# First norm of a frame normalised on ScalarE as one multiply-add a tile, its bias made by GpSimd

## The chip, the cores and the metric

The kernel runs on one core of one Trainium2 chip. The metric is the device time of one execution in microseconds (us); lower is better. Beside the plain runs there is one profiled execution, from which all rows below are taken. Engines are written as the profile writes them: PE is TensorE's matmul side and PEld its weight loads, DVE is VectorE, ACT is ScalarE, POOL is GpSimd, SP is SyncE; "PEq", "ACTq", "SPq" are the sequencers of these engines, which issue DMAs.

## What is computed

A gated cross-attention block with a mixture of experts behind it, on 2 x 1024 tokens of width 256 (2048 rows), against 154 context rows for each batch, 16 heads of 16 columns, 8 experts of which each token takes 2. Cut to what matters here:

```python
def _layernorm(x, eps=1e-05):
    m = jnp.mean(x, axis=-1, keepdims=True); v = jnp.var(x, axis=-1, keepdims=True)
    return (x - m) / jnp.sqrt(v + eps)

# first half: the norm whose normalising step is changed is the inner one here
x = x + jnp.tanh(g_xattn[0]) * attention(_layernorm(x), ctx, ctx, mask, Wq, bq, Wk, bk, Wv, bv, Wo, bo)
# second half: sigmoid router, top 2 of 8 experts, GELU layers 256 -> 1024 -> 256, weighted sum
x = x + jnp.tanh(g_ffn[0]) * experts(_layernorm(x), Wg, W1, b1, W2, b2)
```

## The kernel before

The 2048 rows are 16 tiles of 128 rows; two tiles make a **unit**, so there are U = 8 units, numbered 0 to 7. The program has three stages: a setup (weights turned, keys and values made, first units begun), ten **frames** of attention, and the expert stage, which takes 39 groups of 128 gathered tokens.

Every engine has its own instruction stream, written by hand; semaphores tie them. Nothing is reordered by a compiler, so what stands behind a waiting instruction on its engine waits with it. The loop is `for u in FRAMES: for i in range(ITEMS)` on each engine, with ITEMS = 10 items a frame. Frame u does the softmax of unit u (item i: one pair of heads), the maxima of unit u+1, the output projection and second norm of unit u-1, the router logits of unit u-2, and the first norm and query of unit u+3. The work of several units is so laid side by side in one frame.

The first norm of a unit has three parts. VectorE makes mean and variance (`first_moments`, lines 679 and 682). GpSimd makes 1/sqrt(var + eps) from them by an add and a power (`first_rstd`, lines 379 and 381). VectorE then subtracts the mean and multiplies (`layernorm1`, line 688, two instructions of 128 x 256 a unit), which gives `xn`. TensorE turns `xn` (`turn_x`, line 1088), ScalarE copies the turned tile out (`evacuate_x`, line 508), and TensorE multiplies by the query weights (`query`, line 1096). ScalarE and VectorE write the query's high and low halves (lines 515 and 715), and DMAs stack them for the score matmuls.

Moments and 1/sqrt are made in groups: `FIRST_NORMS = [(0,), (1, 2, 3)] + [(u,) for u in range(4, U)]`. Unit 0 and units 1 to 3 come in the setup; unit u+4 has its 1/sqrt made in frame u, one frame before its norm. `layernorm1` is called in the setup for units 0, 1, 2 and, in frames 0 to 4, at item 4 for units 3 to 7.

GpSimd's stream in the setup, around `first_rstd(1)`, stacks the keys for the scores, eight small DMAs for the high halves and eight for the low ones:

```python
stack_keys(pool, 1, kh, range(8), kst_pool_landed)
first_rstd(1)
pool.wait_ge(kv_made, 2 * KC)
stack_keys(pool, 2, kl, range(8), kst_pool_landed)
load(1)
```

The first score matmul (`max_scores(0, 0)`, line 1075) waits for these (`kst_pool_landed`) and for the query's DMAs (`qst_landed`), which ScalarE issues in the setup behind `evacuate_x(1)` (line 280).

In the frames ScalarE does, item by item, the exponential of the scores (line 583), and between them the copies out of PSUM and the high halves of the expert weights (`weights_high`, line 493); VectorE makes the low halves (`weights_low`, line 788), row maxima (line 722), their negative (`negate_maxima`, line 730), the division by the softmax sums (`weigh_values`, lines 699 and 700), and the residual update (line 878) behind the output projection (line 1246). GpSimd issues the loads of the expert weights (`load`, line 390) and adds the output bias to x (line 420).

Of the kernel before, what the change touches and what calls it, by code (L numbers as in the profile page):

```python
# [12 lines left out]
P = 128  # L13
F32, F16, I32, U8 = mybir.dt.float32, mybir.dt.float16, mybir.dt.int32, mybir.dt.uint8
ALU = mybir.AluOpType
# [11 lines left out]
def build(nc, x, ctx, mask, g_xattn, g_ffn, wq, bq, wk, bk, wv, bv, wo, bo, wg, w1, b1, w2, b2, out):  # L27
# [40 lines left out]
    with es:  # L68
# [46 lines left out]
        with ExitStack() as es_tail:  # L115
            outer, es = es, es_tail
            WT_qo = sb("WT_qo", [P, 2, KC, D])
            outT = sb("outT", [P, 2, 2 * UT])
            attn, attnT = sb("attn", [P, 2, D]), sb("attnT", [P, 2, KC, P])
            xn2 = attn  # L120
            xn2T = attnT
            stats, mv = sb("stats", [P, 2, 6]), sb("mv", [P, 2, 2])
            var, rstd = sb("var", [P, 2]), sb("rstd", [P, 2])
            recip = sb("recip", [P, 2, N_HEADS])


            with ExitStack() as es_attn:
                es = es_attn
                qst_spare = sb("qst2", [P, NPAIR, UT], F16)
                qh, ql = sb("qh", [P, KC, UT], F16), sb("ql", [P, KC, UT], F16)  # L130
                xn = sb("xn", [P, 2, D])
                xnT = xn
                kst = sb("kst", [P, B, NPAIR, 2, SP], F16)
                kst_late.append(sb("kst_late1", [P, NPAIR, 2 * (SP - P)], F16))
                v_a.append(sb("v_a1", [P, N_HEADS, VC]))
                v_b.append(sb("v_b1", [P, 4, 4, VC]))
                qst = [sb(f"qst{i}", [P, NPAIR, UT], F16) for i in range(2)] + [qst_spare]
                mv1, rstd1 = sb("mv1", [P, T, 2]), sb("rstd1", [P, T])
                rowmax, negmax = sb("rowmax", [P, 2 * N_HEADS]), sb("negmax", [P, 2 * N_HEADS])
                negmaxT = sb("negmaxT", [2 * N_HEADS, P], F16)  # L140
                probs = sb("probs", [P, 3, 2, UT])


            with ExitStack() as es_route:
                es = es_route
                ahead = sb("ahead", [P, T, E, E], F16)
                sig, gate_rows, rank = sb("sig", [P, T, E]), sb("gate_rows", [P, T, E]), sb("rank", [P, T, E])
                chosen16, chosen = sb("chosen16", [P, T * E], F16), sb("chosen", [P, TOP_K, T, E])
                sb("first_ranks_end", [P, 8192 - 2048 - 3 * 512 - 256 - 1024], U8)
                at_place, tab_rhs = sb("at_place", [P, TOP_K * T, P], F16), sb("tab_rhs", [P, TOP_K * T, TAB], F16)  # L150
                before, ones = sb("before", [P, P], F16), sb("ones", [P, P], F16)
                iota_slot, iota_tile = sb("iota_slot", [P, P], F16), sb("iota_tile", [P, TAB], F16)
                token_no, spare_row = sb("token_no", [P, TOP_K * T]), sb("spare_row", [P, 1])
                picked = sb("picked", [P, TOP_K, T, E])
                n_int, n_tiles, tile_end, tile_base, no_add = (sb("n_int", [P, E], I32), sb("n_tiles", [P, E]), sb("tile_end", [P, E]),
                                                                sb("tile_base", [P, E]), sb("no_add", [P, E]))
                pos_f, local_f, place_f, base_f, tile_f, place_neg = (sb(n, [P, TOP_K, T]) for n in (
                    "pos_f", "local_f", "place_f", "base_f", "tile_f", "place_neg"))
                token_neg = sb("token_neg", [P, TOP_K * T])
                pos_i, local_i, place_i = (sb(n, [P, TOP_K, T], I32) for n in ("pos_i", "local_i", "place_i"))  # L160
                empty, token_m1 = sb("empty", [P, TAB]), sb("token_m1", [P, TAB])
                past, begun = sb("past", [P, TAB, E], F16), sb("begun", [P, TAB, E], F16)
                expert_f = sb("expert_f", [1, TAB])
                b2_rows = sb("b2_rows", [P, E, D])
            es = outer
# [23 lines left out]
        bo_gated = sem("bo_gated")  # L189
        dve_step = sem("dve_step")  # L190
        ln1_done, x_biased = sem("ln1_done"), sem("x_biased")
        moments1_made, var1_made, rstd1_made = sem("moments1_made"), sem("var1_made"), sem("rstd1_made")
        neg_half_made, v_zeroed = sem("neg_half_made"), sem("v_zeroed")
        moments_made, var_made, rstd_made = sem("moments_made"), sem("var_made"), sem("rstd_made")
# [154 lines left out]
        def _(pool):  # L349
# [25 lines left out]
            def first_rstd(n):  # L375
                units = FIRST_NORMS[n]
                tiles = slice(2 * units[0], 2 * units[-1] + 2)
                pool.wait_ge(moments1_made, n + 1)
                nc.gpsimd.tensor_scalar(var1[:, tiles], mv1[:, tiles, 1], EPS, None, ALU.add).then_inc(var1_made, 1)
                pool.wait_ge(var1_made, n + 1)  # L380
                nc.gpsimd.tensor_tensor(rstd1[:, tiles], var1[:, tiles], neg_half[:, 0:2 * len(units)], ALU.pow).then_inc(rstd1_made, 1)

            pool.wait_ge(neg_half_made, 1)
            first_rstd(0)
# [24 lines left out]
            for n, (_, high, low) in enumerate(chunks):  # L409
# [6 lines left out]
                if n in bias_at:  # L416
                    u = bias_at[n]
                    pool.wait_ge(bo_gated, 1)
                    pool.wait_ge(ln1_done, u + 1)
                    nc.gpsimd.tensor_tensor(x_unit(u), x_unit(u),  # L420
                                            bias_o[:, :].unsqueeze(1).broadcast_to([P, 2, D]), ALU.add).then_inc(x_biased, 1)
                if n < SETUP_CHUNKS:
# [56 lines left out]
        def _(act):  # L479
# [7 lines left out]
            def weights_high(n):  # L487

                if n == E * KC:
                    act.wait_ge(x2_stored, 16 * 3)  # L490
                    pass
                act.wait_ge(w_staged[n % 2], 16 * (n // 2 + 1))
                ins = nc.scalar.activation(chunks[n][1], W_stage[n % 2][:, :], ACT.Copy, scale=W_SCALE)  # L493
                if n < SETUP_CHUNKS:
                    ins = nc.scalar.activation(W_stage[n % 2][:, :], W_stage[n % 2][:, :], ACT.Copy, scale=W_SCALE)
                ins.then_inc(w_high, 1)

            def evacuate_values(v, n):
                act.wait_ge(pv_done, ITEMS * v + 5 * (n + 1))
# [76 lines left out]
            for u in FRAMES:  # L576
                for i in range(ITEMS):
# [16 lines left out]
                    if i == 1 and live(u - 2):  # L594
                        v = u - 2
                        act.wait_ge(q_filled, q_nth["logits", v])
                        nc.scalar.activation(Z[:, 2 * v:2 * v + 2, :].rearrange("p j e -> p (j e)"), Q_BANK[:, 0:2 * E],
                                             ACT.Exp, scale=-1.0).then_inc(q_free, 1)
                    if i == 4 and live(u - 1):
                        v = u - 1  # L600
                        act.wait_ge(a_filled, a_nth["attnT", v])
# [60 lines left out]
        def _(dve):  # L662
# [187 lines left out]
            for u in FRAMES:  # L850
                for i in range(ITEMS):
# [7 lines left out]
                    if i == 3 and live(u - 1):  # L859
# [8 lines left out]
                        for j in range(2 if v == U - 1 else 0):  # L868
                            dve.wait_ge(last_turned, j + 1)
                            weigh_values(j, LAST_TURN[j], xn).then_inc(last_weighed, 1)  # L870
                    if i == 4 and live(u + 3):
                        layernorm1(u + 3)
                    if i == 5 and live(u - 1):
                        v = u - 1
                        dve.wait_ge(q_filled, q_nth["wo", v])
# [127 lines left out]
        def _(pe):  # L1003
# [78 lines left out]

            def turn_x(v):
                a_use("xT", v)
                pe.wait_ge(ln1_done, v + 1)
                for c in range(KC):
                    for j in range(2):
                        ins = nc.tensor.transpose(A_BANK[:, c * UT + j * P:c * UT + (j + 1) * P], xn[:, j, c * P:(c + 1) * P], ident[:, :])
# [300 lines left out]
```

## Time and profile before

| | |
|---|---|
| median of 3 runs | 473.85 us (471.4 to 474.21) |
| the profiled execution | 474.62 us |
| its span, first to last instruction | 472.5 us |
| mean granted TensorE clock | 0.931 |
| busy: PE, DVE, ACT, POOL | 402.3, 313.5, 226.3, 174.6 us |

The setup ends at about 48 us of the span, the frames run from there to about 215 us, routing to 237 us, and the expert stage fills the rest. A row of the timeline gives start, length, engine, line, operation, `out<-in`, how many instructions were merged, and in brackets how long the engine sat idle before it and what released it. The chain is the sequence of work that ended last, traced back from the end.

### The profile page before, as it was taken

Reading aid. Unit: us, or ns where it says so; the run is one execution under the profiler, and the core shown is the slowest. Engines: PE = TensorE matmul, PEld = TensorE weight load, DVE = VectorE, ACT = ScalarE, POOL = GpSimd, SP = SyncE. Lnnn points to the kernel's source line nnn. Section 1 sums busy time; section 2 is a strip of 40 time slices with the busy share of each in tenths; the row PEclk is TensorE's granted clock in tenths of the full one; section 3 lists DMA queues with packets and bytes.
Section 4 is the critical chain, followed back from the end, with each engine's and each line's share of the span. In section 5 each row is a group of like instructions: output and inputs, shape, how many; then the busy total and the mean of one; then the engine's idle time right before and its main releaser. Section 6 shows DMA issues by size and latency. Waiting matters only on the chain.

```text
span 472.5 us, 11085 instructions
## 1 busy us (share of the span) xinstructions
PE 402.3 (85%) x4018; PEld 319.1 (68%) x4018; DVE 313.5 (66%) x833; ACT 226.3 (48%) x576; POOL 174.6 (37%) x193
## 2 busy tenths in 40 slices
PE   5848988988989888975259999999999999999980
PEld 3623445554555544544259999999999999999970
DVE  4666776968777586688826667666666666665650
ACT  2244664656555465646235544544454454443530
POOL 8624642223222131210043444454544445444331
PEclk9985898999999899987559999999999999999996
DMA  7463353525353433442011332322333222233311
GB/s 217 101 184 113 124 155 112 175 100 168 100 163 107 153 108 130 135 141 84 4 52 23 56 57 49 46 47 49 49 54 58 46 51 46 47 49 46 46 24 22
DMA packets 35300, 41.27 MB, mean 87 GB/s; under 512 B 10461, under 2 KB 29777, under 8 KB 35121
## 3 DMA queue, kind: packets, MB, share of 16 engines
q0 software_dynamic: 12608, 27.48, 25.0%
q1 hardware_dynamic: 20113, 12.22, 8.9%
q10 hardware_dynamic: 2528, 0.87, 0.8%
q8 instruction: 33, 0.54, 0.5%
q14 instruction: 18, 0.15, 0.1%
HBM read 26.90 MB, written 9.50 MB: 77 GB/s over the span
## 4 chain that ended last, share of the span: by engine, by line
PE 69%; DVE 15%; DMA 5%; ACT 5%; issue 3%; POOLq 0%; ACTq 0%; SPq 0%; POOL 0%; DVEq 0%
PE bank L1309 7%; PE bank L1310 7%; PE bank L1311 7%; PE bank L1323 7%; PE bank L1324 7%; PE bank L1325 7%; PE bank L1058 6%; PE bank L1075 4%; DVE rowmax L722 3%; PE bank L1246 3%; PE bank L1096 3%; DMA out_rows<-y_sb,scatter_tab 2%; PE bank L1278 2%; DVE W L788 2%; PE bank L1214 2%
## 5 line engine op out<-in xcount | busy, mean ns | idle before, releaser
L1309 PE MATMUL bank<-xh,W 128*128 128x128 f16 x624 | 121.8, 221 | 0.9 <-DVE xl L953 0.9
L1310 PE MATMUL bank<-xl,W 128*128 128x128 f16 x624 | 121.7, 221 | 0.0
L1311 PE MATMUL bank<-xh,W 128*128 128x128 f16 x624 | 121.7, 221 | 0.0
L647 ACT ACTIVATE h<-bank,b1T 128x128 f32<-128x128 f32 x312 | 88.9, 368 | 58.7 <-PE bank L1311 56.1
L459 POOL DMA_INDIRECT out_rows<-y_sb,scatter_tab x39 | 62.2, 1594 | 108.6 <-DVE y_sb L982 99.4
L1323 PE MATMUL bank<-W,hh 128*128 x312 | 85.1, 273 | 1.1 <-DVE hl L964 1.1
L1324 PE MATMUL bank<-W,hh 128*128 x312 | 85.0, 273 | 0.0
L1325 PE MATMUL bank<-W,hl 128*128 x312 | 85.0, 273 | 0.0
L722 DVE TENSOR_REDUCE rowmax<-bank 128x2 f32<-128x308 f32 x128 | 57.1, 472 | 25.7 <-PE bank L1075 24.8
L962 DVE CAST hh<-h 128x512 f16<-128x512 f32 x78 | 33.5, 430 | 47.5 <-ACT h L647 46.7
L1309 PEld LDWEIGHTS bank<-xh,W 128*128 x624 | 61.7, 99 | 4.3 <-DVE xl L953 1.3
L1310 PEld LDWEIGHTS bank<-xl,W 128*128 x624 | 61.7, 99 | 3.4
L583 ACT ACTIVATE probs<-bank 128x512 f32<-128x512 f32 x80 | 47.3, 596 | 32.7 <-PE bank L1180 21.1
L1311 PEld LDWEIGHTS bank<-xh,W 128*128 x624 | 61.7, 99 | 0.0
L964 DVE TENSOR_TENSOR hl<-h,hh 128x512 f16<-128x512 f32 x78 | 54.0, 692 | 2.7
L390 POOL DMA_DIRECT2D W_stage<-in_L_ffn_W x32 | 21.7, 679 | 83.4 <-DVE W L788 82.2
L451 POOL DMA_INDIRECT xg<-xn_scratch,gather_tab x39 | 39.2, 1004 | 35.5 <-DVE gather_tab L940 17.0
L1075 PE MATMUL bank<-kst,qst 97*128 97x308 f16 x128 | 39.9, 329 | 10.1 <-DVE rowmax L722 6.7
L629 ACT ACTIVATE xh<-bank 128x256 f16<-128x256 f32 x39 | 14.9, 383 | 67.4 <-PE bank L1278 67.3
L1058 PE MATMUL bank<-probs,v_a 128*32 128x256 f32 x256 | 40.7, 398 | 4.5 <-ACT probs L583 4.2
L1075 PEld LDWEIGHTS bank<-kst,qst 97*128 97x128 f16 x128 | 12.3, 100 | 35.3 <-DVE rowmax L722 21.8
L788 DVE SCALAR_TENSOR_TENSOR W<-W_stage,W 128x1024 f16<-128x1024 f32 x28 | 34.0, 1218 | 2.9 <-ACT W L493 2.9
(178 smaller groups left out, 655.4 us busy)
## 6 DMA issues: line engine op xcount, KB each, us to landing
W_stage<-in_L_ffn_W POOLq DMA_DIRECT2D x32, 512.0 KB, 4.0
xn_scratch<-attn SPq DMA_DIRECT2D x8, 256.0 KB, 2.2
qst<-qh SPq DMA_DIRECT2D x60, 32.0 KB, 2.4
X_late<-in_x SPq DMA_DIRECT2D x6, 256.0 KB, 6.7
out_rows<-X_late SPq DMA_DIRECT2D x6, 256.0 KB, 2.5
b_rows<-in_L_ffn_b SPq DMA_DIRECT2D x1, 1024.0 KB, 4.8
qst<-ql SPq DMA_DIRECT2D x28, 32.0 KB, 3.1
xg<-xn_scratch,gather_tab POOLq DMA_INDIRECT x39, 2.9
```

What stands on the lines that cost most here:

```text
L459: nc.gpsimd.indirect_dma_start(out=out, out_offset=bass.IndirectOffsetOnAxis(ap=scatter_tab[:, t:t + 1], axis=0), in_=y_sb[t % 3][:, :], i ...
L647: ins = nc.scalar.activation(h32[s % 4][:, m * P:(m + 1) * P], H_BANKS[s % 4][:, m * P:(m + 1) * P], ACT.Gelu_apprx_tanh, scale=1.0 / W_SC ...
L722: nc.vector.reduce_max(rowmax[:, 2 * n:2 * n + 2], S1_BANKS[g % 2][:, 0:2 * S].rearrange("p (a s) -> p a s", a=2), AX_X).then_inc(rowmax_d ...
L964: nc.vector.tensor_tensor(hl[s % 4][:, :], h32[s % 4][:, :], hh[s % 4][:, :], ALU.subtract).then_inc(hl_made, 1)
L1058: ins = nc.tensor.matmul(dst, lhs, rhs, start=(i % 5 == 0 and a == 0), stop=(i % 5 == 4), skip_group_check=True)
L1075: nc.tensor.matmul(S1_BANKS[g % 2][:, 0:2 * S].rearrange("p (a s) -> p a s", a=2), qst[v % 3][0:ROW_MAX, p, j * P:(j + 1) * P], kst[0:ROW_ ...
L1309: nc.tensor.matmul(dst, wh, xh[t % 3][:, cut], start=(c == 0), stop=False)
L1310: nc.tensor.matmul(dst, wh, xl[t % 3][:, cut], start=False, stop=False)
L1311: ins = nc.tensor.matmul(dst, wl, xh[t % 3][:, cut], start=False, stop=(c == KC - 1))
L1323: nc.tensor.matmul(y, hh[s % 4][:, cut], both[0], start=(m == 0), stop=False)
L1324: nc.tensor.matmul(y, hh[s % 4][:, cut], both[1], start=False, stop=False)
L1325: ins = nc.tensor.matmul(y, hl[s % 4][:, cut], both[0], start=False, stop=(m == FC - 1))
```

## The change

For units 3 to 7, the units that are normalised in the frames, the normalising step leaves VectorE (item 4) and becomes two ScalarE activations a unit behind the exponential of item 2: Identity(rstd * x + shift), with shift = -mean * rstd, one multiply-add a tile of 128 x 256. GpSimd makes shift: in each of the five `first_rstd` calls that hold such a unit it gets two operations more, a negation of the means and a product with rstd. Units 0 to 2 are normalised by VectorE as before. The waits for the finished norm follow the new semaphore.

```diff
+                mean_neg, shift1 = sb("mean_neg", [P, T]), sb("shift1", [P, T])
...
@@ -377,8 +379,14 @@
                 tiles = slice(2 * units[0], 2 * units[-1] + 2)
                 pool.wait_ge(moments1_made, n + 1)
                 nc.gpsimd.tensor_scalar(var1[:, tiles], mv1[:, tiles, 1], EPS, None, ALU.add).then_inc(var1_made, 1)
+                if units[-1] >= 3:
+                    nc.gpsimd.tensor_scalar(mean_neg[:, tiles], mv1[:, tiles, 0], -1.0, None, ALU.mult).then_inc(mean_negated, 1)
                 pool.wait_ge(var1_made, n + 1)
                 nc.gpsimd.tensor_tensor(rstd1[:, tiles], var1[:, tiles], neg_half[:, 0:2 * len(units)], ALU.pow).then_inc(rstd1_made, 1)
+                if units[-1] >= 3:
+                    pool.wait_ge(rstd1_made, n + 1)
+                    pool.wait_ge(mean_negated, sum(m[-1] >= 3 for m in FIRST_NORMS[:n + 1]))
+                    nc.gpsimd.tensor_tensor(shift1[:, tiles], mean_neg[:, tiles], rstd1[:, tiles], ALU.mult).then_inc(shift1_made, 1)
 
             pool.wait_ge(neg_half_made, 1)
             first_rstd(0)
@@ -416,7 +424,10 @@
                 if n in bias_at:
                     u = bias_at[n]
                     pool.wait_ge(bo_gated, 1)
-                    pool.wait_ge(ln1_done, u + 1)
+                    if u < 3:
+                        pool.wait_ge(ln1_done, u + 1)
+                    else:
+                        pool.wait_ge(ln1_late_done, u - 2)
                     nc.gpsimd.tensor_tensor(x_unit(u), x_unit(u),
                                             bias_o[:, :].unsqueeze(1).broadcast_to([P, 2, D]), ALU.add).then_inc(x_biased, 1)
                 if n < SETUP_CHUNKS:
@@ -494,6 +505,14 @@
                 if n < SETUP_CHUNKS:
                     ins = nc.scalar.activation(W_stage[n % 2][:, :], W_stage[n % 2][:, :], ACT.Copy, scale=W_SCALE)
                 ins.then_inc(w_high, 1)
+
+            def first_norm(v):
+                act.wait_ge(q_filled, q_nth["q", v - 1])
+                act.wait_ge(shift1_made, sum(m[-1] >= 3 for m in FIRST_NORMS[:first_norm_of[v]]))
+                for j in range(2):
+                    t = 2 * v + j
+                    ins = nc.scalar.activation(xn[:, j, :], x_unit(v)[:, j, :], ACT.Identity, scale=rstd1[:, t:t + 1], bias=shift1[:, t:t + 1])
+                ins.then_inc(ln1_late_done, 1)
 
             def evacuate_values(v, n):
                 act.wait_ge(pv_done, ITEMS * v + 5 * (n + 1))
@@ -596,6 +615,8 @@
                         act.wait_ge(q_filled, q_nth["logits", v])
                         nc.scalar.activation(Z[:, 2 * v:2 * v + 2, :].rearrange("p j e -> p (j e)"), Q_BANK[:, 0:2 * E],
                                              ACT.Exp, scale=-1.0).then_inc(q_free, 1)
+                    if i == 2 and live(u + 3):
+                        first_norm(u + 3)
                     if i == 4 and live(u - 1):
                         v = u - 1
                         act.wait_ge(a_filled, a_nth["attnT", v])
@@ -868,8 +889,6 @@
                         for j in range(2 if v == U - 1 else 0):
                             dve.wait_ge(last_turned, j + 1)
                             weigh_values(j, LAST_TURN[j], xn).then_inc(last_weighed, 1)
-                    if i == 4 and live(u + 3):
-                        layernorm1(u + 3)
                     if i == 5 and live(u - 1):
                         v = u - 1
                         dve.wait_ge(q_filled, q_nth["wo", v])
@@ -1082,7 +1101,10 @@
 
             def turn_x(v):
                 a_use("xT", v)
-                pe.wait_ge(ln1_done, v + 1)
+                if v < 3:
+                    pe.wait_ge(ln1_done, v + 1)
+                else:
+                    pe.wait_ge(ln1_late_done, v - 2)
                 for c in range(KC):
                     for j in range(2):
                         ins = nc.tensor.transpose(A_BANK[:, c * UT + j * P:c * UT + (j + 1) * P], xn[:, j, c * P:(c + 1) * P], ident[:, :])
```

Three places show what stands in each stream; names before `<-` are tiles written, behind it those read.

GpSimd in the setup, from the stacking of the high key halves (`kst<-kh`) to the next weight load, first before, then changed:

```order
L269 DMA kst<-kh 16x4x154 x8
L379 TENSOR_SCALAR var<-mv 128x6
L381 TENSOR_TENSOR rstd<-var,neg_half 128x6
L269 DMA kst<-kl 16x4x154 x8
L390 DMA W_stage<-in_L_ffn_W 128x1024
```

```order
L271 DMA kst<-kh 16x4x154 x8
L381 TENSOR_SCALAR var<-mv 128x6
L383 TENSOR_SCALAR mean_neg<-mv 128x6
L385 TENSOR_TENSOR rstd<-var,neg_half 128x6
L389 TENSOR_TENSOR shift<-mean_neg,rstd 128x6
L271 DMA kst<-kl 16x4x154 x8
L398 DMA W_stage<-in_L_ffn_W 128x1024
```

One operation now stands ahead of the power and one between it and the eight DMAs of the low key halves.

ScalarE in frame 2, from the weight piece of item 0 to the exponential of item 4 (`probs<-bank` is an exponential, `Z<-bank` the router's), first before, then changed:

```order
L493 ACTIVATE W<-W_stage 128x1024
L583 ACTIVATE probs<-bank 128x512
L597 ACTIVATE Z<-bank 128x16
L583 ACTIVATE probs<-bank 128x512 x2
L493 ACTIVATE W<-W_stage 128x1024
L583 ACTIVATE probs<-bank 128x512
```

```order
L504 ACTIVATE W<-W_stage 128x1024
L602 ACTIVATE probs<-bank 128x512
L616 ACTIVATE Z<-bank 128x16
L602 ACTIVATE probs<-bank 128x512
L514 ACTIVATE xn<-X_late,shift,rstd 128x256 x2
L602 ACTIVATE probs<-bank 128x512
L504 ACTIVATE W<-W_stage 128x1024
L602 ACTIVATE probs<-bank 128x512
```

The pair of the norm stands between the exponentials of items 2 and 3, which were neighbours.

VectorE in frame 2, items 3 to 5, first before, then changed:

```order
L730 TENSOR_SCALAR negmax<-rowmax 128x32
L699 RECIPROCAL recip<-bank 128x16
L700 TENSOR_TENSOR attn<-bank,recip 128x256
L699 RECIPROCAL recip<-bank 128x16
L700 TENSOR_TENSOR attn<-bank,recip 128x256
L688 TENSOR_SCALAR xn<-X_late,mv,rstd 128x256 x2
L788 SCALAR_TENSOR_TENSOR W<-W_stage,W 128x1024
L878 SCALAR_TENSOR_TENSOR X_early<-bank,tanh_g,X_early 128x512
```

```order
L751 TENSOR_SCALAR negmax<-rowmax 128x32
L720 RECIPROCAL recip<-bank 128x16
L721 TENSOR_TENSOR attn<-bank,recip 128x256
L720 RECIPROCAL recip<-bank 128x16
L721 TENSOR_TENSOR attn<-bank,recip 128x256
L809 SCALAR_TENSOR_TENSOR W<-W_stage,W 128x1024
L897 SCALAR_TENSOR_TENSOR X_early<-bank,tanh_g,X_early 128x512
```

The weight piece follows the division directly; nothing ahead of it has moved.

## Rows read from the trace of the kernel before

**Rows 1.** Stretches of two frames: busy us (instructions), granted clock, DMA share, GB/s

```profile
68.00:89.00 21.00, 18.36 (x109) 10.70 (x109) 16.17 (x39) 11.35 (x20) 5.10 (x9) 0.92 0.46 139
89.00:110.00 21.00, 18.56 (x127) 11.57 (x125) 16.43 (x40) 12.78 (x24) 4.98 (x9) 1.00 0.42 135
```

**Rows 2.** The chain that ended last in frame 3: start, length, what

```profile
118.05 0.43 DVE attn L700
...
120.14 1.94 PE bank L1246 x8
```

**Rows 3.** Timeline of VectorE in frames 0, 1 and 3

```profile
63.34 0.48 DVE L722 TENSOR_REDUCE rowmax<-bank 128x2 f32<-128x308 f32 x1 [1.93 <-PE bank L1075]
...
79.97 0.75 DVE L878 SCALAR_TENSOR_TENSOR X_early<-bank,tanh_g,X_early 128x512 f32<-128x512 f32 x1 [3.50 <-PE bank L1246]
...
118.39 0.72 DVE L688 TENSOR_SCALAR xn<-X_late,mv,rstd 128x256 f32<-128x256 f32 x2
...
122.10 0.75 DVE L878 SCALAR_TENSOR_TENSOR X_late<-bank,tanh_g,X_late 128x512 f32<-128x512 f32 x1 [1.85 <-PE bank L1246]
```

**Rows 4.** Timeline of ScalarE: exponential of item 3 in frames 0, 1, 4

```profile
53.57 0.60 ACT L583 ACTIVATE probs<-bank 128x512 f32<-128x512 f32 x1 [0.55 <-PE bank L1180]
...
71.59 0.60 ACT L583 ACTIVATE probs<-bank 128x512 f32<-128x512 f32 x1 [1.56 <-PE bank L1180]
...
136.44 0.60 ACT L583 ACTIVATE probs<-bank 128x512 f32<-128x512 f32 x1 [1.42 <-PE bank L1180]
```

**Rows 5.** ScalarE's groups by line and shape: busy us, mean ns

```profile
L515 ACT ACTIVATE qh<-bank,bias_q 128x256 f16<-128x256 f32 x16 | 6.7, 471 | 10.3 <-DMA qst<-ql 8.1 <-PE bank L1096 2.2
...
L528 ACT ACTIVATE at_place<-at_place,token_no,token_neg 128x128 f16<-128x128 f16 x12 | 4.8, 482 | 0.0
...
L608 ACT ACTIVATE at_place<-iota_slot,place_neg 128x128 f16<-128x128 f16 x12 | 3.6, 388 | 3.0 <-DVE local_f L765 3.0
```

**Rows 6.** Timeline of ScalarE: the query's high halves in frame 3

```profile
127.92 0.83 ACT L515 ACTIVATE qh<-bank,bias_q 128x256 f16<-128x256 f32 x2
```

**Rows 7.** Timeline of PE in frame 0, at the turn of the maxima

```profile
57.00 0.27 PE L1107 MATMUL bank<-ident,negmax 128*32 128x128 f32 x1 [0.72 <-DVE negmax L730]
```

**Rows 8.** Timeline of GpSimd in the setup

```profile
20.45 0.27 POOL L379 TENSOR_SCALAR var<-mv 128x6 f32<-128x6 f32 x1
20.80 1.36 POOL L381 TENSOR_TENSOR rstd<-var,neg_half 128x6 f32<-128x6 f32 x1
22.13 4.28 POOL L269 DMA_DIRECT2D kst<-kl  x8
```

**Rows 9.** Timeline of VectorE in the setup: the norm of unit 1

```profile
22.27 0.73 DVE L688 TENSOR_SCALAR xn<-X_early,mv,rstd 128x256 f32<-128x256 f32 x2 [2.43 <-POOL rstd L381]
```

**Rows 10.** The chain from unit 1's norm to the first score matmul

```profile
21.30 1.73 PE bank L1144 x8
...
23.15 0.64 PE bank L1088 x4
...
26.03 3.85 DMA qst<-ql
...
29.93 0.32 PE bank L1075
```

**Rows 11.** Tile kst, the last key DMA (`kst<-kl`) alone: time to landing

```profile
DMA to landing us min/median/max: 3.8/3.8/3.8
```

**Rows 12.** Tile negmax (ns min/median/max), then timelines of VectorE and GpSimd

```profile
L730 DVE TENSOR_SCALAR negmax<-rowmax x8: 180/181/1302, 43.8 to 181.2; 128x32 f32<-128x32 f32 x8
...
55.55 1.30 DVE L730 TENSOR_SCALAR negmax<-rowmax 128x32 f32<-128x32 f32 x1
...
55.53 1.27 POOL L420 TENSOR_TENSOR X_early<-X_early,bias_o 128x512 f32<-128x512 f32 x1
...
116.33 0.72 POOL L381 TENSOR_TENSOR rstd<-var,neg_half 128x2 f32<-128x2 f32 x1
```

**Rows 13.** The chain in frame 1: the output projection

```profile
76.73 3.22 PE bank L1246 x8
```

More of the change, by code:

```diff
@@ L191, in build @@
         ln1_done, x_biased = sem("ln1_done"), sem("x_biased")
+        mean_negated, shift1_made, ln1_late_done = sem("mean_negated"), sem("shift1_made"), sem("ln1_late_done")
         moments1_made, var1_made, rstd1_made = sem("moments1_made"), sem("var1_made"), sem("rstd1_made")
```

## The prediction

> **What bounds the kernel now.** I read the chain of work that ended last first, to see which engine's work sets the end of a frame; then the timelines of VectorE and ScalarE at the two places that the change touches, to see what each waits for there; then GpSimd's timeline in the setup, since two of the new operations stand ahead of DMAs. The ten frames run at about 21 us each [rows 1]. In frame 3 the chain goes over VectorE's division, PE's output projection and back to VectorE's residual update [rows 2]. PE is busy 18.4 to 18.6 of 21 us in these stretches, VectorE 16.2 to 16.4 and ScalarE 11.4 to 12.8 [rows 1], and no engine is full: what counts is each hand-over. Everything up to the expert stage is one chain, so a delay that lies on it moves the end by its own length, and one that lies beside it by nothing. The reader is to see in the rows that both the place that loses the norm and the place that gains it are places where the engine waits for PE.
>
> **VectorE loses ten instructions.** Five pairs, 0.72 us a pair as it stands in the timeline [rows 3], the one at 118.39: 5 x 0.72 = 3.6 us less of VectorE's work. In frame 3 only the weight piece and the residual update come behind it, and the update finds VectorE idle for 1.85 us until PE's output projection ends; in frame 1 it is 3.50 us [rows 3]. The projection hangs on the division, which ends at 118.48 [rows 2] and stands ahead of the norm. So the idle time grows from 1.85 to about 2.6 us and nothing else starts earlier but the weight piece and the weight load behind it. Frame 0 has no division; there the next wait for PE behind the norm is 1.93 us [rows 3]. Gain: 0, in all five frames. What would be late next if the norm did count is the same projection, so nothing is hidden behind it.
>
> **ScalarE gains ten instructions.** No row shows this form (two operands by partition, 128 x 256). The nearest one with two such operands is 128 wide and takes 482 ns; with one operand it is 388 ns at 128 wide and 471 ns at 256 [rows 5], so 128 columns more cost 83 ns. One instruction: 482 + 83 = 565 ns. Two in a row overlap: 2 x 471 = 942 ns are 0.83 us in the timeline [rows 6], 0.11 us less. The pair: 2 x 565 - 110 = 1020 ns, and the next instruction waits some 0.11 us less than that, so ScalarE is held for 0.9 to 1.0 us. The bounds are 0.83 us (the query's pair, one operand fewer) and 1.2 us (565 ns each with no overlap, rounded up). It stands where ScalarE waits for PE: before the exponential of item 3 ScalarE is idle for 1.56 us in frame 1 and 1.42 us in frame 4 [rows 4], frames 2 and 3 lying between. In these four frames 1.42 - 1.2 leaves at least 0.2 us even at the upper bound: cost 0. In frame 0 the idle time is 0.55 us [rows 4], so that exponential comes 0.3 to 0.65 us late, 0.4 taken. What waits for it is PE's value matmul of item 4 and then the turn of the maxima, before which PE is idle for 0.72 us, waiting for VectorE's negation [rows 7]. Cost in frame 0: 0, up to 0.1 if the end of the range and all hand-overs add up. None of the waits that the new pair adds is late: its shift was made one frame earlier (unit 3's in the setup), and the query before it ended in the frame before.
>
> **GpSimd gains ten instructions.** In the frames GpSimd's own next step is a weight load that waits for VectorE's low half, so its two small operations (0.27 us is the one at 128 x 6 [rows 8]) cost nothing there. In the setup they stand in the way twice.
>
> First, the negation comes between the add and the power. The add starts at 20.45 and the power at 20.80, with 0.35 us between them for a 0.27 us operation and its semaphore [rows 8]. The negation fills part of that gap: two operations at some 0.21 us each reach to 20.87, with the semaphore at most to 21.07. The power and all behind it come 0.07 to 0.27 us later, 0.13 taken. VectorE's norm of unit 1 waits for the power (2.43 us [rows 9]) and ends at 23.00; PE's turn starts at 23.15, 0.15 us behind, and its previous matmul ended at 23.03 [rows 10]. So PE's turn was tied to both, and now follows the norm: the chain is 0.13 us later at ScalarE's four DMAs of the query's low half, the last of which lands at 26.03 + 3.85 = 29.88, and PE's first score matmul starts at 29.93 [rows 10].
>
> Second, the product stands ahead of the eight DMAs of the low key halves. It takes between 0.27 us (the add at the same shape) and 1.36 us (the power at the same shape) [rows 8]; a product is nearer to the add, and with its semaphore I take 0.4. These DMAs come 0.13 + 0.4 = 0.5 us later, 0.3 to 1.7 at the bounds. The eight were issued from 22.13 on in 4.28 us [rows 8], the last of them at 22.13 + 7/8 x 4.28 = 25.9; it landed 3.8 us later [rows 11], at 29.7, 0.2 us before the query's. Now it lands at 30.2, where the query's lands at 30.0. PE's first score matmul goes from 29.93 to about 30.25: cost 0.3 us. Bounds: 0.1 (the queues are full at that time and the 512 KB weight load behind comes later too, which may give it back) and 1.5 (1.7 - 0.2).
>
> **The sum.** 0 on VectorE, 0 on ScalarE, +0.3 in the setup: 474.62 + 0.3 = 474.9 us against the profiled execution. That execution lies 0.8 us above the median of the runs, 473.85, so the forecast for a median is 473.85 + 0.3 = 474.15, rounded to **474.2 us**. A measurement of this kernel can hardly tell less than 1% (4.7 us) from no change, since its three runs lie 2.8 us apart.
>
> **The rivals.**
>
> *Slower: the key DMAs set the start of the scores.* It is the second step of the setup at its upper end. If the product on GpSimd costs what the power does, 1.36 us, the DMAs come about 1.65 us later and land 1.45 us behind the query's. Every tenth from the point where the delay passes 0.2 us is a tenth on the end: 474.2 - 0.3 + 1.5 = 475.4. For it: the slack is only 0.2 us [rows 10, 11]. Against: a power is a long operation by itself. Chance 0.1.
>
> *Slower: GpSimd in VectorE's way.* In the one place where VectorE's negation (0.18 us in the median of its eight) was to start beside GpSimd's bias operation, at 55.55, it took 1.30 us and ended with that operation [rows 12]. In frames 1 to 3 the power now ends about when the negation starts: in frame 3 at 117.05 [rows 12], ahead of the division at 117.43 to 118.48 [rows 2]. The product now follows it there. If the negation or the division waits for it, that is up to 0.27 us in three frames, +0.8: 475.0. Against: only a part of a GpSimd operation on two columns can be memory access. The Trainium skill, "GPSIMD Engine Reference", 1. Specifications, says that GpSimd's SBUF interfaces are shared with VectorE and contended for by VectorE instructions in a two-port mode or with two SBUF inputs; by that rule the negation could wait and the division, which reads PSUM, could not, and the row at 55.55 agrees. Chance 0.08.
>
> *Faster by chance of place.* The stop at 55.55 cost 1.30 - 0.18 = 1.1 us on the chain, and it came about because GpSimd's bias began 0.02 us earlier [rows 12]. And the output projection took 3.22 us in frame 1 against 1.94 in frame 3 [rows 2, 13], in a stretch at a granted clock of 0.92 instead of 1.00 [rows 1]: 1.3 us. A shift of some tenths ahead of them can undo one of the two: 474.2 - 1.2 = 473.0. It can as well make a new one, +1.3: 475.5. Chances 0.08 and 0.04.
>
> *Faster: VectorE's relief counts.* If the frames were paced by VectorE's total work and not by its hand-overs, 5 x 0.72 = 3.6 us would go: 470.6. The idle times of 1.85 to 3.50 us speak against it [rows 3]. Chance 0.04.
>
> *Slower by over 1%: ScalarE's hole is not there.* If each exponential of item 3 were late by the whole pair, 5 x 1.0 = 5 us: 479.2. It would need PE's score matmul of item 3 to come 1.4 us earlier than now, which nothing in the change brings. The Trainium skill, "ScalarE: Activation LUTs", Rules for kernel authors, says to use VectorE and not ScalarE for additions and products; per tile it is right here (VectorE's pair is 0.72 us, the estimate for ScalarE's 1.02), and it would decide the time only in this case. Chance 0.03.
>
> **How the numbers follow.** The forecast has 0.63. Inside 1% (469.4 to 478.9, taking the forecast for zero) lie all cases but the last; with 0.03 on each side for what I have not seen: faster 0.03, same 0.92, slower 0.05. For the range I take the two slow cases up to 475.5 and the fast one at 473.0, and widen both ends by the scatter of a median of such runs, since one of three lay at 471.4: 472.2 to 475.8. The relief case at 470.6 and the hole case stay out, 0.07 together, and some 0.1 for scatter.
>
> **What the changed profile would show.** VectorE's busy time falls by some 3.6 us and its idle time ahead of the residual updates grows by 0.7 us each. ScalarE's busy time rises by 5.6 us (ten of 565 ns); ahead of the exponential of item 3 some 0.4 to 0.6 us of idle time are left in frames 1 to 4 and none in frame 0. The first score matmul starts at 30.1 to 30.5 us instead of 29.93, released by a key DMA. Frame 3 has its length of before. The prediction is wrong if the frames shorten or stretch by themselves, above all if PE's turn of the maxima or the exponentials now wait for an engine that they did not wait for.

## The result, and the profile after

The kernel after takes 470.36 us (median of 6 runs, 469.88 to 471.83), the kernel before, beside it, 473.55 us (6 runs, 471.4 to 474.43): a ratio of 0.9941, 95% interval 0.9916 to 0.9966. A second comparison (12 and 35 runs) gave 0.9972, 0.9944 to 1.0000. Both intervals hold a gain of 0.34 to 0.56%, 1.6 to 2.7 us. The ratios are those of the comparisons; the quotient of two medians can differ from them by 0.1%. The forecast was 474.2 us, the range from 472.2 on. The profiled execution after took 470.21 us with a span of 468.5 us, against 474.62 and 472.5.

VectorE's timeline in frame 3 after the change, then ScalarE's in frames 0, 1 and 3.

```profile
117.05 1.21 DVE L809 SCALAR_TENSOR_TENSOR W<-W_stage,W 128x1024 f16<-128x1024 f32 x1
120.76 0.75 DVE L897 SCALAR_TENSOR_TENSOR X_late<-bank,tanh_g,X_late 128x512 f32<-128x512 f32 x1 [2.50 <-PE bank L1268]
```

```profile
51.65 1.08 ACT L514 ACTIVATE xn<-X_late,shift,rstd 128x256 f32<-128x256 f32 x2
52.64 0.58 ACT L602 ACTIVATE probs<-bank 128x512 f32<-128x512 f32 x1
...
70.48 0.60 ACT L602 ACTIVATE probs<-bank 128x512 f32<-128x512 f32 x1 [0.58 <-PE bank L1202]
...
112.74 1.08 ACT L514 ACTIVATE xn<-X_late,shift,rstd 128x256 f32<-128x256 f32 x2
114.27 0.60 ACT L602 ACTIVATE probs<-bank 128x512 f32<-128x512 f32 x1 [0.45 <-PE bank L1202]
```

These answer to [rows 3, 4]. VectorE's idle time ahead of the residual update grew from 1.85 to 2.50 us, and what ends it is still PE's projection. ScalarE's pair takes 1.08 us, and 0.58 us of its hole are left in frame 1, 0.45 us in frame 3, none in frame 0. Frame 3, from the residual update at 99.57 to that at 120.76, took 21.19 us, as before.

GpSimd's timeline in the setup, then the chain there ([rows 8, 10]):

```profile
19.43 0.28 POOL L381 TENSOR_SCALAR var<-mv 128x6 f32<-128x6 f32 x1
19.78 0.25 POOL L383 TENSOR_SCALAR mean_neg<-mv 128x6 f32<-128x6 f32 x1
20.01 1.36 POOL L385 TENSOR_TENSOR rstd<-var,neg_half 128x6 f32<-128x6 f32 x1
21.45 0.21 POOL L389 TENSOR_TENSOR shift<-mean_neg,rstd 128x6 f32<-128x6 f32 x1
21.67 4.18 POOL L271 DMA_DIRECT2D kst<-kl  x8
```

```profile
24.98 3.73 DMA qst<-ql
28.71 0.05 issue
28.75 0.32 PE bank L1094
```

The power follows the add by 0.58 us instead of 0.35. The query's DMA is still what the first score matmul waits for: it landed at 28.71 us, the last key DMA at 28.55, where the kernel before had 29.88 and 29.72.

**Where the 4.0 us of the two spans went.** I cut both traces at the same events. The rows are the start of GpSimd's first key DMA, of the first score matmul, of the first exponential, of the residual updates of frames 1 to 8, and of the first expert's turn:

```
stretch ending at   key  score  exp   f1    f2    f3    f4    f5    f6    f7    f8   turn  end
before            16.31 13.62 18.99 31.05 20.94 21.19 20.84 23.08 20.20 18.53 12.60 22.90 232.25
after             15.29 13.46 18.98 31.01 20.83 21.19 20.84 21.19 20.33 18.53 12.69 22.16 232.00
```

A frame's length here is the time from one residual update to the next. The first 1.0 us lies ahead of every changed instruction; that stretch ran from 15.07 to 17.14 us in the 18 profiles of this case, and is chance. Frames 1 to 4, in which the norm was moved out, are alike to 0.11 us. The routing stretch that ends at the turn is 0.74 us shorter; over the 18 profiles it took either 22.2 us or 22.7 to 23.1, and the kernel before had both, 22.90 here and 22.16 in a later profile. The one large difference is frame 5, 1.89 us, in which no norm stood. Here is the chain in it, before and then after:

```profile
159.08 0.04 DVE negmax L730
159.12 0.40 issue
159.52 0.27 DVE recip L699
...
161.00 0.92 PE bank L1233 x4
161.92 0.57 PE bank L1185 x3
162.49 1.00 PE bank L1058 x4
163.49 2.51 PE bank L1246 x8
```

```profile
157.74 0.04 DVE negmax L751
157.78 0.06 issue
157.84 0.26 DVE recip L720
...
159.31 0.63 PE bank L1255 x4
159.94 0.34 PE bank L1207 x4
160.28 0.56 PE bank L1077 x4
160.83 1.94 PE bank L1268 x8
```

Before, 0.40 us of "issue" stand between the negation and the reciprocal, time in which VectorE waited for nothing that the profile shows; after, 0.06. Frame 3 of the kernel before has 0.06 there too:

```profile
117.05 0.04 DVE negmax L730
117.09 0.06 issue
117.14 0.26 DVE recip L699
```

So PE, which waits for the division behind the reciprocal, is idle for longer in frame 5, and its four steps behind that take 5.0 us instead of 3.5. PE's timeline, before and then after:

```profile
161.00 0.92 PE L1233 MATMUL bank<-ident,attn 128*128 128x128 f32 x4 [1.70 <-DVE attn L700]
```

```profile
159.31 0.63 PE L1255 MATMUL bank<-ident,attn 128*128 128x128 f32 x4 [1.34 <-DVE attn L721]
```

### The profile page after: what moved, and what is told of

It is laid out like the page before. It is cut to its first block, busy times and chain, and to the rows that moved or that the text cites. A ratio compares the mean times of both kernels' runs of the same rounds, so it can differ in the third digit from the quotient of the medians.

```text
span 468.5 us, 11100 instructions
## 1 busy us (share of the span) xinstructions
PE 398.3 (85%) x4018; PEld 315.6 (67%) x4018; DVE 308.8 (66%) x823; ACT 230.9 (49%) x586; POOL 177.6 (38%) x203
## 4 chain that ended last, share of the span: by engine, by line
PE 64%; DVE 16%; DMA 7%; ACT 4%; issue 4%; POOL 2%; POOLq 0%; ACTq 0%; SPq 0%; DVEq 0%
PE bank L1331 7%; PE bank L1332 7%; PE bank L1333 7%; PE bank L1345 7%; PE bank L1347 7%; PE bank L1346 7%; PE bank L1077 5%; PE bank L1268 3%; PE bank L1094 3%; DVE rowmax L743 3%; PE bank L1118 3%; DMA out_rows<-y_sb,scatter_tab 2%; PE bank L1300 2%; DMA W_stage<-in_L_ffn_W 2%; DVE W L809 1%
```

## The experiments

There are four theories. **Place**: VectorE stops for 0.34 us at fixed places of its instruction stream, counted in instructions from its start; in the kernel before one of these places falls on frame 5's reciprocal, on the chain, and the change moved it off. **Relief**: the work that VectorE lost counts. **GpSimd**, **ScalarE**: their new work counts.

### First four: the two kernels again, and each side alone

c_before and c_after are unchanged. pool_only adds GpSimd's ten operations to the kernel before and leaves the norms on VectorE. dve_out leaves the norms of units 3 to 7 out of the kernel before; these units' `xn` is what stood there, and the two waits for their norms are lowered to that for unit 2 (not shown):

```diff
-                    if i == 4 and live(u + 3):
-                        layernorm1(u + 3)
```

> The kernel before, unchanged, as a second sample of itself. In the profile of before, frame 5 is 1.9 us longer than after (VectorE stands still for 0.3 us between its negation and the division, and PE then runs at half the clock for a stretch), and the first 15 us, ahead of every changed instruction, are 1.0 us longer. Theory of chance: these two belong to one execution; this profile shows other values, ratio 1.000 +- 0.003, and the change's 3 us are partly of this kind. Theory of place: they are tied to the program; this profile shows frame 5 with the same stop and the same half clock, at 23.1 us from residual update to residual update.

> The changed kernel, unchanged, as a second sample. If the gain is the kernel's own, ratio 0.993 to 0.995 again, and frame 5 again 21.2 us without the stop. If it was chance, 0.997 to 1.000.

> The kernel before with only GpSimd's ten new operations; VectorE's norms stay. My theory that the gain comes from VectorE's stream (its ten instructions, or where they stand) gives 1.000 to 1.002 (+0 to +0.8 us). The rival, that the gain comes from GpSimd's later key DMAs and weight load (less crowding at the first score matmul), gives 0.995 to 0.998 and a first score matmul that starts earlier than in before.

> The kernel before with the normalising step of units 3 to 7 left out altogether (these units' xn is what the last query left there); no work is added anywhere. If VectorE's relief is the cause, ratio 0.992 to 0.995, as the full change. If the ten instructions on VectorE cost nothing, 0.998 to 1.001, and the frames 1 to 4 keep their 21.2 and 20.9 us.

Measured: c_before 1.0028 (1.0004 to 1.0052), c_after 0.9972 (0.9944 to 1.0000), pool_only 1.0012 (0.9982 to 1.0043), dve_out 0.9952 (0.9926 to 0.9978). That the kernel before stands 0.28% from itself shows what such an interval is worth. By the ratios alone the expectations would have misled: c_after fell where its text put chance, and dve_out, at 0.9952, outside the 0.998 to 1.001 that it gave for a norm that costs nothing. dve_out takes as many instructions out of VectorE's stream as the change does. The frames tell more. Frame 5 took 23.05 us in c_before and 23.03 in pool_only, each with the stop; 21.20 in c_after and dve_out, without. Frames 2 to 4 of dve_out (20.85, 21.21, 20.83 us) equal those of c_before (20.94, 21.21, 20.84): with the norm wholly gone they get no shorter, but for 0.09 us in frame 2, which is explained below. Relief is out; GpSimd costs nothing that can be seen.

### Moving the stream without moving work

before_pad10 keeps the norms on VectorE and adds ten instructions of one column in the setup, where VectorE waits for PE:

```diff
+            for j in range(10):
+                nc.vector.memset(idle[:, j:j + 1], 0.0)
             for n in range(2 * NPAIR):
```

after_pad10, after_pad14 and after_pad15 add 10, 14 and 15 of them to the kernel after, before_pad1 one to the kernel before.

> The kernel before with ten instructions of one column each added on VectorE in the setup, where it waits 3.4 us for the first score matmul; nothing is taken away, and the norms stay on VectorE. Place theory (what the change gained is that VectorE's stop of 0.26 us between negmax and recip in frame 5, after which PE waits 1.70 us and runs at half clock for a stretch, is met elsewhere in the stream when the number of VectorE instructions ahead of it is another): the stop leaves that place, frame 5 takes 21.2 us instead of 23.05, and the kernel is about 1.9 us faster than before (ratio 0.996) though it does more work. Relief theory (the ten instructions count by their own time): frame 5 stays at 23.05 us, ratio 1.000 to 1.001.

Measured: 471.63 us against 473.05, ratio 0.9963 (0.9937 to 0.9989), frame 5 21.20 us. VectorE does more than before, and frame 5 loses its 1.85 us. This decides for the place as the cause of frame 5's length. The median agrees: it gains as much as c_after did. Of the medians in the first three groups, the five kernels without the stop (c_after, dve_out, before_pad10, after_pad10, after_late_shift) have 471.57 to 472.36 us, the three with it (c_before, pool_only, before_act) 473.49 to 474.04. In VectorE's timeline the reciprocal follows 0.10 us behind the negation:

```profile
156.37 0.18 DVE L731 TENSOR_SCALAR negmax<-rowmax 128x32 f32<-128x32 f32 x1
156.47 0.25 DVE L700 RECIPROCAL recip<-bank 128x16 f32<-128x16 f32 x1
```

> The kernel after with the same ten one-column instructions added on VectorE in the setup, so that from frame 5 on its instructions have the numbers in the stream that they have before; ScalarE's norms, GpSimd's operations and VectorE's relief stay. Place theory: the stop of 0.26 us between negmax and recip in frame 5 is back, frame 5 takes 23.05 us instead of 21.2, ratio to before about 1.000. Relief theory: frame 5 stays at 21.2 us, ratio 0.994 to 0.997 as for the kernel after.

Measured: 0.9977 (0.9949 to 1.0006), frame 5 21.21 us. The place theory's number was missed. The count was mine to mend: a norm takes three instructions from the stream, one of them only a wait for its second semaphore. VectorE has 1085 records in the trace of the kernel before and 1070 in that of the kernel after.

> The kernel after with fifteen one-column instructions added on VectorE in the setup. The norm of a unit is two instructions and one more for its second semaphore, so the change takes three from VectorE's stream a norm, fifteen in all, and with ten added the count was not restored: the run with ten says nothing against the place theory. With fifteen, VectorE's instructions from frame 5 on have the numbers in the stream that they have before, while ScalarE's norms, GpSimd's operations and VectorE's relief stay. Place theory by this count: the stop of 0.26 us between negmax and recip in frame 5 is back, PE waits 1.70 us there, frame 5 takes 23.05 us, and the ratio to before is 1.000 within 0.002: the change by itself is worth nothing. Relief theory, or a place theory with another count: frame 5 stays at 21.2 us, ratio 0.994 to 0.998.

Measured: 472.85 us against 473.18, ratio 1.0005 (0.9970 to 1.0039). The stop is back on the reciprocal:

```profile
157.10 0.18 DVE L752 TENSOR_SCALAR negmax<-rowmax 128x32 f32<-128x32 f32 x1
157.54 0.26 DVE L721 RECIPROCAL recip<-bank 128x16 f32<-128x16 f32 x1 [0.26 <-issue]
```

With before's places no gain of the change is left in the median, though the interval is too wide to exclude one of 0.3%. And frame 5 took 21.55 us, not 23.05: the stop itself was there and cost its 0.35 us, but PE did not go to half clock, of which more below.

> The same with fourteen: everything on VectorE stands one place earlier in the stream than in the kernel before. Place theory: the stop falls on the next instruction, the division behind the reciprocal, where 0.1 to 0.34 us of it can be seen between the two; frame 5 takes 21.3 to 23.0 us. Relief theory: 21.2 us and no gap but the usual 0.04 us between the two.

> The kernel before with one one-column instruction added on VectorE in the setup: all of its stream stands one place later. Place theory: the stop falls on the instruction ahead of the reciprocal of frame 5, the wait for a semaphore between negmax and recip, so that recip still starts late by up to 0.34 us, or not at all if the stop hides beside negmax; frame 5 takes 23.05 us or 21.2 us. Two such runs show how narrow the place is. Relief theory: 23.05 us, since nothing is taken away.

Measured in after_pad14: the gap falls on the division behind the reciprocal, 0.10 us more than its usual 0.28 from start to start; frame 5 21.30 us.

```profile
159.04 0.25 DVE L721 RECIPROCAL recip<-bank 128x16 f32<-128x16 f32 x1
159.42 0.42 DVE L722 TENSOR_TENSOR attn<-bank,recip 128x256 f32<-128x256 f32 x1
```

In before_pad1 frame 5 is at 21.20 us, and the stop stands in frame 2, on the reciprocal there. VectorE's timeline, and PE's behind it:

```profile
94.08 0.18 DVE L731 TENSOR_SCALAR negmax<-rowmax 128x32 f32<-128x32 f32 x1
94.52 0.26 DVE L700 RECIPROCAL recip<-bank 128x16 f32<-128x16 f32 x1 [0.26 <-issue]
```

```profile
96.01 0.63 PE L1236 MATMUL bank<-ident,attn 128*128 128x128 f32 x4 [1.70 <-DVE attn L701]
...
97.69 3.40 PE L1249 MATMUL bank<-WT_qo,attnT 128*128 128x256 f32 x8
```

Frame 2 took 22.84 us, which its expectation did not name. In c_before the first reciprocal of frame 2 starts at 94.32 and its division at 94.70, 0.10 us late as in after_pad14. So the kernel before has two such places: on frame 2's division and on frame 5's reciprocal. Counted from 0 in VectorE's records of the trace, waits for semaphores included, they are numbers 191 and 319, 128 apart, and all 18 profiles follow: the place costs 0.34 us where it falls on the reciprocal, 0.10 on the division, and nothing on the wait ahead of the reciprocal. In the kernel after they fall on other instructions, at which no gap shows. Only these two places were seen. At number 447, 128 further on, no instruction came late: in the kernel before, an instruction of the routing (it writes `local_i`) started 0.09 us behind its predecessor there, as it does in the kernel after at number 432.

### ScalarE's pair and GpSimd's setup

before_act adds the pair of activations to the kernel before, into a tile that nobody reads; after_late_shift emits unit 3's negation and product behind the eight DMAs `kst<-kl` and the weight load.

> The kernel before with a pair of two-operand activations of 128 x 256 added on ScalarE at item 2 of frames 0 to 4, where the kernel after has its norm; they write a tile that nobody reads, and VectorE's norms stay. It shows what the pair costs by itself. Prediction's theory (hidden in ScalarE's holes): ratio 1.000, frames 2 to 4 as before (20.94, 21.19, 20.84 us), frame 5 at 23.05 us since VectorE's stream is unchanged. Rival (the pair makes PE's pause in frame 1 longer or later, and PE goes to half clock for a stretch): exponential 0 to residual update of frame 1 takes 31.0 us, as in both profiles of the kernel after, where the kernel before had 29.5 us in one of two: about 1.5 us slower, ratio 1.003.

> The kernel after with GpSimd's negation and product for unit 3 moved behind the eight DMAs of the low key halves and the weight load, so that GpSimd's road to these DMAs is that of before. Prediction's theory (the two stand on the path to the first score matmul for 0.3 us): the stretch from GpSimd's first key DMAs to the first score matmul is 0.3 us shorter than in the kernel after, ratio to before 0.9935 where after has 0.994 to 0.997. Rival (the first score matmul waits for the query's DMA, which they do not delay): no difference, the stretch stays at 13.5 to 14.0 us.

Measured: before_act 1.0001 (0.9980 to 1.0022), frames 2 to 4 at 20.93, 21.20, 20.83 us: the pair is free. Frame 1 took 31.11 us, as the rival had it, but before_again, with nothing added, took 31.12. Of 18 profiles 7 have the long frame 1 (31.0 to 31.2 us, the others 29.5 to 29.7), 4 of 9 with the norms on VectorE and 3 of 8 with them on ScalarE: chance. after_late_shift: 0.9974 (0.9947 to 1.0001) where c_after had 0.9972. Its power follows the add by 0.36 us, and its eight DMAs `kst<-kl` start 5.86 us behind the first key DMA, as in the kernel before (5.82; 6.38 in the kernel after), yet the first score matmul came 15.19 us behind the first key DMA, since the query's DMA took longer:

```profile
25.11 5.37 DMA qst<-ql
30.48 0.05 issue
30.53 0.45 PE bank L1102
```

That DMA took 3.7 to 5.7 us from run to run, and hides a term of 0.3 us. Neither do the medians settle it, since their intervals are 1.3 us wide to each side. What the traces do show is that the query's DMA landed last in all 18 profiles, 0.09 to 2.2 us behind the last key DMA.

### Why 0.34 us cost 1.9

after_delay and before_delay (on before_pad10) put one VectorE instruction of 0.35 us ahead of frame 5's reciprocal:

```diff
+                        if u == 5:
+                            nc.vector.tensor_scalar(late[:, :], bias_v_pad[:, :], pad_mask[:, 0:1], None, ALU.mult)
```

> The kernel after with one VectorE instruction of about 0.3 us (128 x 256, into a tile that nobody reads) between negmax and recip of frame 5 alone. It puts a delay of the stop's length at the stop's place without the stop. Theory of two steps (the stop makes PE's pause 1.70 us instead of 1.34, PE then goes to half clock for a stretch, and this is most of the cost): frame 5 takes 22.7 to 23.1 us though the delay is only 0.3 us, ratio to before 0.998 to 1.000. Rival (the cost of 1.87 us belongs to the stop itself): frame 5 takes 21.5 us, PE at full clock, ratio 0.995 to 0.998.

> The kernel before_pad10 (no stop in frame 5, norms on VectorE) with one VectorE instruction of 0.35 us between negmax and recip of frame 5. If a longer pause of PE (1.6 us instead of 1.34) is what brings the half clock, with the norms on VectorE, frame 5 takes 22.7 to 23.0 us; if it is chance or needs more than the pause, 21.5 us as in the kernel after with the same delay.

> The kernel after_pad15 once more, for a second profile. The stop of 0.26 us between negmax and recip in frame 5 is there again (place theory). What is asked is PE's clock behind it: if VectorE's norms on the engine before were what made PE's half clock follow the pause of 1.70 us, frame 5 takes 21.5 us again; if it is chance, 23.0 us is as likely.

> The kernel before_pad1 once more. Place theory: the stop of 0.26 us stands in frame 2 again and not in frame 5; frame 2 takes 22.8 us if the half clock follows the pause again, 21.3 us if that is chance; frame 5 takes 21.2 us.

> The kernel before once more. Place theory: the stop stands in frame 5, as in all four profiles of kernels with before's VectorE stream so far; frame 5 takes 23.05 us if the half clock follows a pause of 1.70 us there always, 21.5 us if it is chance.

Measured: after_delay 0.9980 (0.9945 to 1.0015), frame 5 21.46 us at full clock, where the theory of two steps had 22.7 to 23.1; before_delay 23.00 us at half clock, as that theory has it; after_pad15_b 21.55; before_again 21.56; before_pad1_b frame 2 at 23.07, frame 5 at 21.20. Windows of frame 5, c_before (159 to 164) and before_again (160 to 165); the columns are the stretch, its length, busy us of the five engines, granted clock, DMA share, GB/s:

```profile
159.00:164.00 5.00, 4.50 (x19) 2.79 (x20) 1.48 (x2) 1.17 (x2) 0.75 (x1) 0.66 0.30 102
```

```profile
160.00:165.00 5.00, 4.27 (x27) 3.12 (x28) 2.43 (x4) 1.76 (x4) 0.75 (x1) 1.00 0.28 89
```

Both have the stop and PE's idle time of 1.70 us behind it; one has a clock of 0.66, the other 1.00. Over all profiles, frame 5: with PE idle for 1.61 to 1.70 us, half clock (1.2 GHz) for a stretch in 5 of 9; with 1.34 to 1.44 us, in 0 of 9. In frame 2 with 1.70 us, 2 of 2. So the delay costs its own length always, and some 1.5 us more in 7 of these 11 cases.

What decides between the two is open. c_before and before_again are one kernel and fell apart, so chance has a part in it. But of the 11 cases the half clock followed in 7 of the 8 with the norms on VectorE and in none of the 3 with them on ScalarE (after_delay, after_pad15, after_pad15_b); after_delay and before_delay, alike there but for the norms and the added instructions in the setup, fell apart too. That the moved norm itself makes the half clock rarer is a rival that three profiles can't exclude. Frame 1 speaks against it: PE is idle for 1.58 to 1.60 us before the turn of the divided values there in all 18 profiles, and its half clock came about as often on both sides, as counted above. So does the ratio of 1.0005 of after_pad15, within its wide interval.

## Why the prediction was wrong

- **"Gain: 0, in all five frames" for VectorE's lost work held**: before's idle time took it, as worked out, 2.50 us where about 2.6 was forecast, and dve_out shows it with the norm gone altogether. Frames 1 to 3 of the kernel after are as long as before or shorter, so GpSimd's product was not in VectorE's way there either.
- **The step that failed is the pricing of VectorE's ten instructions by their time alone**, with "nothing else starts earlier" but the weight piece. The sum had no term for where the rest of VectorE's stream comes to stand once instructions are taken out ahead of it; that term was put at nothing without a reason. The row was there: 0.40 us of "issue" on the chain in frame 5, where frame 3 has 0.06, and a frame of 23.08 us beside others of 21. I took the chain in frame 3 to stand for that of all later frames. The term: 23.08, 23.05, 23.03, 23.08 and 21.56 us in the five profiles with before's stream, 22.76 in the mean, against 21.20 without the stop, 1.56 us; with the two profiles of after_pad15, which have the stop too, it is 1.2 us. In 3 of the 9 profiles without stop or delay the half clock came in frame 6 instead (21.3 to 21.4 us against 20.2), 0.4 us in the mean; with a stop or delay it did so only in after_delay, at full clock in frame 5. That leaves 0.8 to 1.2 us; c_after, before_pad10, after_pad10 and after_late_shift measured 0.7 to 1.5 us between medians. The rest of the 3.2 us of the first comparison has no place that I could show, and the second does not repeat it. The routing stretch may hold a part: it was the long one in 6 of 9 profiles with the norms on VectorE and in 1 of 8 with them on ScalarE, but also in dve_out, and no run was made on it.
- **The rival "faster by chance of place"** had the kind right, with a chance of 0.08. It named two other places, and neither was the cause; where it touches the truth, that is luck. The negation's stop in frame 0 did go (1.30 us to 0.18), but it is worth little: from the first exponential to frame 1's update took 29.63 us with a negation of 1.42 us (dve_out) and 29.46 us with one of 0.56 (c_before). Frame 1's half clock came in 7 of 18 profiles, on both sides.
- **ScalarE's pair**: 1.08 us against 1.02 forecast, cost 0 [rows 4 to 6]; before_act confirms it. Its holes kept 0.45 and 0.58 us, 0.4 to 0.6 forecast. The 5.6 us more of busy time counted the overlap of a pair twice; it grew by 4.6 us, from 226.3 to 230.9.
- **GpSimd in the setup**: the product was 0.21 us with 0.08 ahead of it, inside the bounds; the negation delayed the power by 0.23 instead of 0.13; the key DMAs came 0.56 us later in their stretch, 0.5 forecast. The +0.3 us at the first score matmul did not come. It assumed that the last key DMA keeps its 3.8 us; counted from the first key DMA, the last one landed at 13.26 us after and at 13.41 before, though it was issued later. The query's DMA stayed last, and its own scatter is larger than the term.
- **The chances**: with 0.03 taken off on each side, the cases give same 0.91 and slower 0.06, not 0.92 and 0.05. Nothing hangs on it.

## What to carry to other kernels

An edit that takes instructions from an engine's stream or adds some moves every later one; look for unexplained "issue" on the chain, in every frame and not in one, and ask what stands there after the edit. Before a gain of some 0.3% is credited to an edit, time the old kernel with some idle instructions added where its engine waits: here ten of them alone gained as much as the edit. A delay of PE can count for more than its length where it makes an idle time longer that PE's clock had so far survived: here 0.3 us cost some 1.9 in 7 of 11 cases and only its own length in the others. So take more than one profile before a half-clock stretch is credited to an edit.

## What the runs showed of the hardware

VectorE stood still for 0.34 us at two places 128 instructions apart in its stream, waits for a semaphore counted; at the place another 128 further on nothing showed. One instruction more or less decided whether it was seen: on a reciprocal behind its wait 0.34 us, on the next instruction 0.10, one place later none. What it does there no run shows.

PE's granted clock fell to 1.2 GHz behind an idle time of 1.61 to 1.70 us in 7 of 11 cases (frames 2 and 5), behind one of 1.58 to 1.60 us in 7 of 18 (frame 1), and behind one of 1.34 to 1.44 us at the same place of frame 5 in none of 9.
